# A hardware loop over pairs of quads and 64x64 blocks in the output stage of a gated delta rule

## The reference

```
q = l2norm(q) / sqrt(D); k = l2norm(k)
def step(state, inp):
    q_t, k_t, v_t, a_t, b_t = inp
    state = a_t[..., None, None] * state
    stored = einsum('bhij,bhj->bhi', state, k_t)
    delta = b_t[..., None] * (v_t - stored)
    state = state + einsum('bhi,bhj->bhij', delta, k_t)
    o_t = einsum('bhij,bhj->bhi', state, q_t)
_, outs = scan(step, state0, (qT, kT, vT, aT, bT))
var = mean(out * out, axis=-1)
out = out * rsqrt(var + 1e-06) * rms_w
gate = silu(x @ Wgate)
return out * gate @ Wout
```

## Time and profile before

| | |
|---|---|
| median of three runs | 4024.93 us |
| profiled execution | 4019.74 us |
| its span | 4018.1 us |
| TensorE matmul busy, of the span | 2600.4 us, 65% |
| VectorE, ScalarE, POOL busy | 50%, 33%, 19% |
| mean granted clock of TensorE | 0.722 |

### The profile page before, as it was taken

One profiled execution on the slowest core, in us unless ns is written; L12 is line 12 of the kernel. 1 busy time (PEld: TensorE's weight loads), 2 busy tenths in 40 slices (PEclk: granted clock), 3 DMA queues, 4 the chain that ended last, 5 costly groups with the idle time before them and its releaser, 6 DMA issues. The chain is left out here.

```text
span 4018.1 us, 107610 instructions
## 1 busy us (share of the span) xinstructions
PE 2600.4 (65%) x42132; PEld 1917.5 (48%) x42132; DVE 2017.4 (50%) x5379; ACT 1331.4 (33%) x3117; POOL 780.0 (19%) x1137
## 2 busy tenths in 40 slices
PE   5986776246888845555476278778783009999900
PEld 2554544234555534443244256555562009999900
DVE  3385665734666622225502367667767004444466
ACT  3764454224666633332200043333431002222200
POOL 1221112013555510000000011011110660000066
PEclk8987777555555556667676588888995559999955
DMA  3536474663444434442196721211210522222265
GB/s 109 188 129 244 160 259 169 237 239 95 98 107 98 102 97 146 136 128 107 75 415 248 285 103 56 67 56 55 70 48 33 182 95 66 70 70 70 68 202 167
DMA packets 386623, 537.35 MB, mean 134 GB/s; under 512 B 121244, under 2 KB 314744, under 8 KB 378488
## 3 DMA queue, kind: packets, MB, share of 16 engines
q1 hardware_dynamic: 307672, 343.88, 26.0%
q0 software_dynamic: 58304, 152.42, 11.4%
q10 hardware_dynamic: 20320, 36.44, 2.4%
HBM read 327.58 MB, written 216.15 MB: 135 GB/s over the span
## 5 line engine op out<-in xcount | busy, mean ns | idle before, releaser
L1036 ACT ACTIVATE ss_write_ps<-ss_state,ss_gammas 128x64 f32<-128x64 f32 x1024 | 263.3, 303 | 197.5 <-DVE ss_state L1084 197.5
L448 PE MATMUL dc_rows_ps<-dc_weights,dc_hT 128*128 128x512 f32 x512 | 287.8, 691 | 7.3 <-issue 2.6
L2628 PE MATMUL se_up_ps<-se_xT,se_w 128*128 128x128 f32 x2176 | 267.1, 277 | 0.0
L505 PE MATMUL dc_solve_ps<-dc_sides,dc_blocks 32*32 32x32 f32 x8192 | 124.6, 227 | 216.0 <-ACT dc_blocks L599 101.7
L2636 PE MATMUL se_y_ps<-se_w,se_aT 128*128 128x256 f32 x1088 | 257.3, 380 | 0.0
L2628 PEld LDWEIGHTS se_up_ps<-se_xT,se_w 128*128 128x128 f32 x2176 | 255.6, 193 | 0.4 <-DVE se_w L2693 0.3
L2766 POOL DMA_INDIRECT cb_y<-scratch_ys,cb_to x128 | 137.3, 1073 | 564.9 <-DVE cb_to L2780 526.2
L505 PEld LDWEIGHTS dc_solve_ps<-dc_sides,dc_blocks 32*32 32x32 f32 x8192 | 111.5, 139 | 230.0 <-issue 116.5
L2693 DVE COPY se_w<-mx_weights 128x2048 f32 x136 | 166.8, 1227 | 104.1 <-issue 104.1
L2636 PEld LDWEIGHTS se_y_ps<-se_w,se_aT 128*128 128x128 f32 x1088 | 196.8, 191 | 20.7
L1203 PE MATMUL do_mix_ps<-do_u,do_blocks 32*32 32x16 f32 x8192 | 102.5, 196 | 159.3 <-issue 124.0
(11 more groups left out here) (347 smaller groups left out, 5717.2 us busy)
## 6 DMA issues: line engine op xcount, KB each, us to landing
ex_w<-in_w_all SPq DMA_DIRECT2D x64, 1024.0 KB, 21.1
scratch_rows<-dc_rows POOLq DMA_DIRECT2D x64, 512.0 KB, 4.3
scratch_vw<-dc_out POOLq DMA_DIRECT2D x64, 512.0 KB, 4.2
dc_c_rows<-scratch_rows SPq DMA_DIRECT2D x64, 384.0 KB, 4.5
scratch_xs<-wa_zeros ACTq DMA_DIRECT2D x34, 512.0 KB, 14.6
se_xs<-scratch_xs SPq DMA_DIRECT2D x136, 128.0 KB, 2.1
scratch_ys<-se_y SPq DMA_DIRECT2D x136, 128.0 KB, 1.7
ss_wq_rows<-scratch_vw SPq DMA_DIRECT2D x128, 128.0 KB, 2.3
```

The source lines that it names most:

```text
L448: mm = pe.matmul(to, hT[n % 2][:, k, :], weights[:, k, columns], start=(k == 0), stop=(k == HALVES - 1), skip_group_check=True)
L505: mm = pe.matmul(solve_ps[tokens, :].rearrange("p (a f) -> p a f", a=2)[:, :, h * HEAD:(h + 1) * HEAD], blocks[c % 2][tokens, h, :, :].rea ...
L1036: ins = act.activation(write_ps[b][:, k, 0:WIDTH], state[b][:, k, :], ACT.Copy, scale=gammas[i][:, b, k, c:c + 1])
L2628: mm = pe.matmul(up_ps[i % 2][:, c * P:(c + 1) * P], w[i % (2 * AHEAD)][:, k * DFF + c * P:k * DFF + (c + 1) * P], xT[i % 2][:, k, :], sta ...
```

## The change

The stage's blocks become 64x64: a block holds the products of four chunks on its diagonal. A buffer `blocks` keeps one quad's blocks in the layout partition, tile, chunk of the four, token, head, so that one head's block is read with a step of 16 elements. VectorE sets both buffers to zero once. After that eight DMAs for each quad (one for each chunk of a tile, 16 partitions each) write the products straight into the diagonal, and nothing else is ever written. ScalarE's `make_blocks` and the parity mask go. The mix has 128 matmuls in a quad.

For this the delta stage stores the products with the head innermost: its last product writes into a new tile `qkd_turned` with a step of 16 elements, after the previous group's store of that tile.

`read` gets a semaphore of its own, and is loaded behind the blocks. TensorE's program runs over pairs of quads: for each batch of 8 quads the first pair is written out, and the other three are a hardware loop. `weights_ready` is waited for once, ahead of the first mix. A counter `mix_begun` is incremented in each mix.

```diff
         qkd = sb("qkd", [P, PAIRS])
+        qkd_turned = sb("qkd_turned", [P, T, T, HEADS])
...
-                        sync.wait_ge(qkd_out, 16 * g)
+                        sync.wait_ge(qkd_ready, at(g))
...
-                        pool.dma_start(chunk_rows(d["qkd"], g), qkd[:, :]).then_inc(qkd_out, 16)
+                        pool.dma_start(chunk_rows(d["qkd"], g), qkd_turned[:, :, :, :].rearrange("p s t h -> p (s t h)")).then_inc(qkd_out, 16)
...
-                        seq_b.tell(vec.tensor_tensor(rows_of_pairs(qkd), rows_of_pairs(qkd), over_rows(1), ALU.mult), qkd_ready, g + 1)
+                        if g > 0:
+                            vec.wait_ge(qkd_out, 16 * g)
+                        seq_b.tell(vec.tensor_tensor(qkd_turned[:, :, :, :].rearrange("p s t h -> p s h t"), rows_of_pairs(qkd), over_rows(1), ALU.mult), qkd_ready, g + 1)
...
-        qkd = [sb(f"qkd{i}", [P, Q, DIM]) for i in both]
+        blocks = [sb(f"blocks{i}", [P, Q, SIDE, T, HEADS]) for i in both]
...
-        blocks = [sb(f"blocks{i}", [P, 2, HEADS, 2, T]) for i in both]
...
                     if q >= 2:
                         sync.wait_ge(mixed, at((q - 1) * 2))
+                    sync.dma_start(u[i][:, :, :], quad_rows(d["solved_u"], q)).then_inc(first_in[i], 16)
+                    if q < 2:
+                        sync.wait_ge(cleared, at(q + 1))
+                    for c in range(P // T):
+                        lines = slice(c * T, (c + 1) * T)
+                        sync.dma_start(blocks[i][lines, :, c % SIDE, :, :].rearrange("p n t h -> p n (t h)"), quad_rows(d["qkd"], q)[lines, :, :]).then_inc(first_in[i], 16)
+                    if q >= 2:
                         sync.wait_ge(summed, at((q - 1) * 2))
-                    sync.dma_start(qkd[i][:, :, :], quad_rows(d["qkd"], q)).then_inc(first_in[i], 16)
-                    sync.dma_start(u[i][:, :, :], quad_rows(d["solved_u"], q)).then_inc(first_in[i], 16)
-                    sync.dma_start(read[i][:, :, :], quad_rows(d["solved_q"], q)).then_inc(first_in[i], 16)
+                    sync.dma_start(read[i][:, :, :], quad_rows(d["solved_q"], q)).then_inc(read_in[i], 16)
...
-                def mix(m):
-                    q, half = divmod(m, 2)
+                def mix(pair_of_quads, i, half):
+                    m = pair_of_quads * 4 + i * 2 + half
                     if half == 0:
-                        pe.wait_ge(first_in[q % 2], at((q // 2 + 1) * 48))
-                    pe.wait_ge(blocks_ready, at(m + 1))
-                    if m >= 2:
+                        pe.wait_ge(first_in[i], at((pair_of_quads + 1) * FIRSTS))
+                    if not (isinstance(m, int) and m < 2):
                         pe.wait_ge(summed, at(m - 1))
+                    pe.sem_inc(mix_begun, 1)
                     for n in range(2):
                         for h in range(HEADS):
-                            for j in range(4):
-                                tokens = slice(32 * j, 32 * j + 32)
-                                mm = pe.matmul(mix_ps[m % 2][tokens, n, h * HEAD:(h + 1) * HEAD], blocks[m % 2][tokens, n, h, :, :].rearrange("p c t -> p (c t)"),
-                                               u[q % 2][tokens, half * 2 + n, h * HEAD:(h + 1) * HEAD], start=True, stop=True, skip_group_check=True)
+                            for j in range(P // (SIDE * T)):
+                                tokens = slice(SIDE * T * j, SIDE * T * (j + 1))
+                                mm = pe.matmul(mix_ps[half][tokens, n, h * HEAD:(h + 1) * HEAD], blocks[i][tokens, half * 2 + n, :, :, h].rearrange("p c t -> p (c t)"),
+                                               u[i][tokens, half * 2 + n, h * HEAD:(h + 1) * HEAD], start=True, stop=True, skip_group_check=True)
                     mm.then_inc(mixed, 1)
...
-                def project(m):
-                    pe.wait_ge(weights_ready, at(1))
+                def project(q, half, b):
+                    m = q * 2 + half
                     pe.wait_ge(oT_ready, at(m + 1))
-                    if m >= 2:
+                    if not (isinstance(m, int) and m < 2):
                         pe.wait_ge(x_ready, at(m - 1))
...
-                for q in range(QUADS + 1):
-                    if q < QUADS:
-                        mix(2 * q)
-                        mix(2 * q + 1)
-                    if q > 0:
-                        turn(2 * q - 2)
-                        turn(2 * q - 1)
-                        project(2 * q - 2)
-                        project(2 * q - 1)
+                def finish(q, i, b):
+                    for half in range(2):
+                        turn(q, i, half)
+                    for half in range(2):
+                        project(q, half, b)
+
+                def two_quads(ii, b_before, b):
+                    for half in range(2):
+                        mix(ii, 0, half)
+                    if b_before is not None:
+                        finish(ii * 2 - 1, 1, b_before)
+                    for half in range(2):
+                        mix(ii, 1, half)
+                    finish(ii * 2, 0, b)
+
+                pe.wait_ge(weights_ready, at(1))
+                for b in range(BATCH):
+                    first = b * QUADS_PER_BATCH // 2
+                    two_quads(first, b - 1 if b > 0 else None, b)
+                    with pe.Fori(first + 1, first + QUADS_PER_BATCH // 2) as ii:
+                        two_quads(ii, b, b)
+                finish(QUADS - 1, 1, BATCH - 1)
...
-                def make_blocks(m):
-                    q, half = divmod(m, 2)
-                    if half == 0:
-                        act.wait_ge(first_in[q % 2], at((q // 2 + 1) * 48))
-                    if m >= 2:
-                        act.wait_ge(mixed, at(m - 1))
-                    for par in range(2):
-                        ins = act.activation(blocks[m % 2][:, :, :, par, :].rearrange("p n h t -> p (n h) t"),
-                                             pair_of(qkd[q % 2], half).rearrange("p (a t) -> p a t", t=T), ACT.Copy, scale=parity[:, par:par + 1])
-                    ins.then_inc(blocks_ready, 1)
...
-                make_blocks(0)
-                make_blocks(1)
...
-                    if q + 1 < QUADS:
-                        make_blocks(2 * q + 2)
-                        make_blocks(2 * q + 3)
...
+                for i in both:
+                    vec.memset(blocks[i][:, :, :, :, :], 0.0).then_inc(cleared, 1)
...
+                    if half == 0:
+                        vec.wait_ge(read_in[q % 2], at((q // 2 + 1) * 16))
```

More of the change, by code:

```diff
@@ L1108, in build_delta_outputs @@
     Q = 4
+    SIDE = 4
     QUADS = TILES // Q
@@ L1117, in build_delta_outputs @@
         ident = sb("ident", [P, P])
-        parity = sb("parity", [P, 2])
         w_out = sb("w_out", [P, HALVES, DIM])
@@ L1135, in build_delta_outputs @@
         y_ps = [ps(f"y_ps{i}", [P, 2, DIM]) for i in both]
-        consts, order, weights_ready, blocks_ready, mixed, summed, squared, var_ready, rooted, silued, o_ready = map(sem, (
-            "consts", "order", "weights_ready", "blocks_ready", "mixed", "summed", "squared", "var_ready", "rooted", "silued", "o_ready"))
-        turned, oT_ready, projected, x_ready = map(sem, ("turned", "oT_ready", "projected", "x_ready"))
-        first_in, gate_in, x_in = ([sem(f"{n}{i}") for i in both] for n in ("first_in", "gate_in", "x_in"))
+        consts, order, weights_ready, cleared, mixed, summed, squared, var_ready, rooted, silued, o_ready = map(sem, (
+            "consts", "order", "weights_ready", "cleared", "mixed", "summed", "squared", "var_ready", "rooted", "silued", "o_ready"))
+        turned, oT_ready, projected, x_ready, mix_begun = map(sem, ("turned", "oT_ready", "projected", "x_ready", "mix_begun"))
+        first_in, read_in, gate_in, x_in = ([sem(f"{n}{i}") for i in both] for n in ("first_in", "read_in", "gate_in", "x_in"))
         x_out = [sem.from_zero(f"x_out{i}") for i in both]
-        CONSTS = 16 * (4 + BATCH)
+        CONSTS = 16 * (3 + BATCH)
+        FIRSTS = 16 * (P // T + 1)
         def quad_rows(dram, q):
@@ L1213, in turn @@
                         for k in range(HALVES):
-                            mm = pe.transpose(tr_ps[m % 2][:, n, k, :], o[q % 2][:, half * 2 + n, k * P:(k + 1) * P], ident[:, :])
+                            mm = pe.transpose(tr_ps[half][:, n, k, :], o[i][:, half * 2 + n, k * P:(k + 1) * P], ident[:, :])
                     mm.then_inc(turned, 1)
-                def project(m):
-                    pe.wait_ge(weights_ready, at(1))
+                def project(q, half, b):
+                    m = q * 2 + half
@@ L1219, in project @@
                     pe.wait_ge(oT_ready, at(m + 1))
-                    if m >= 2:
+                    if not (isinstance(m, int) and m < 2):
                         pe.wait_ge(x_ready, at(m - 1))
-                    b = m * BATCH // PAIRS_OF_TILES
                     for n in range(2):
```

(2 more changed lines are left out.)

3 lines of the change are left out of this document (1 added, 2 removed).

## The result

The kernel after takes 3985.71 us (median of 4 runs, 3984.70 to 3990.84) beside 4025.15 of before (4015.74 to 4027.43): ratio 0.9909, 95% interval 0.9891 to 0.9927. That is 39 us faster. The forecast was 17 us faster, 4008 us. Its direction held, and the time lies in its range of 3965 to 4050, but the gain is more than twice the one forecast. The profiled execution took 3984.70 us, its span 3983.1.

A forecast was written before the change was run, and what follows sets the result against it. It took the mix to be bound by its program's arrival, about 3.9 us per packet. Terms of -20 (14 periods), -1 (first mixes), +2 (start) and +2 (delta stage) gave -17 us, so 4008 us, range 3965 to 4050.

The forecast's parts named there:

- item 2: Mix on TensorE: 128 rounds a quad at 118 ns, set by strided weight loads whatever the clock, 15.2 us.
- item 4: Projection on TensorE: runs at either clock, taken as 4.9 us, bounds 3.5 and 6.8.
- item 1: TensorE's loop and halved mixing instructions: instruction loads leave the path, taken at zero; straight-part loads of 8.5 us stay hidden.
- item 3: ScalarE without make_blocks: the copy follows the turn at once, turn to projection 2.08 instead of 3.85 us.
- item 7: Delta stage: products writing with a 64-byte stride cost +2 us (0 to +21), the price being mostly for strided reads.
- the filling: Small term added to the mix in the sum of one period, 0.1 us.
- The first two mixes: Start of the output stage: they take 30.5 in place of 31.52 us, -1.
- the start: Start of the output stage: memsets and eight issues delay the constants about 7 us, 1 kept; together +2 (0 to +7).
- A: Rival on the mix: stride costs nothing, mix 9.0 us, period 16.1, about 3910 us; chance 0.11.
- B: Rival on the mix: two row groups' strided loads obstruct each other, 236 ns a round, about 4248 us; 0.16 with milder forms.
- C: Rival: loop back edges load code (+24) or a wait takes the gain, 4020 to 4035 us; chance 0.10.

The follow-up runs named there:

- before, copies first: Kernel before, with ScalarE copying the turned tile ahead of making the next quad's blocks instead of behind it; 3990.99 us, ratio 0.9935.
- after, passes put back: Kernel after, with ScalarE's four former block-making passes again ahead of the copies of the turned tile, writing a spare buffer; 4029.16 us, ratio 1.0028.
- the constants first: Kernel after, with SyncE issuing ident, w_out, rms_w and ga ahead of the first quad's loads; 3971.91 us, ratio 0.9880.
- the turning on the read: Kernel after with those constants loaded first, and VectorE's last delta-stage product reading qkd over the 64-byte stride and writing contiguous; 3965.24 us, ratio 0.9879.

## Why the prediction was right in its direction and its gain too small

Two steps failed: the price of a round in item 2, 118 ns where 110 was measured, and item 4, which set the projection's time apart from the wait in front of it, 4.9 us where 4.49 was measured. The mechanisms of items 1, 2 and 3 held. Here is one period by its parts, each from its start to the next part's start, as a mean over the 14 periods, in us:

| | before | forecast | after | before, copies first | after, passes put back |
|---|---|---|---|---|---|
| mix | 14.27 | 15.3 | 14.19 | 14.72 | 14.19 |
| turn, to the projection | 4.09 | 2.1 | 1.80 | 2.11 | 3.20 |
| projection, to the mix | 5.40 | 4.9 | 4.49 | 4.85 | 6.30 |
| period | 23.76 | 22.3 | 20.47 | 21.68 | 23.69 |

The mix of the kernel after is no shorter than that of before. Halving the instructions took the packets off its path, and the stride put nearly the same time back. Of the 3.29 us that a period gained, 2.29 lie between turn and projection and 0.91 in the projection.

*The instruction loads* (item 1) were right. There are 14 packets in the 14 periods, none of them in the second and third pass of either loop, and the mix shows no gap for any; the form of the loop does not matter, but the halved count does. (Before has 16 quads of 272 matmuls and transposes in this stage, 4352, and not the 4288 given above.)

*The mix* (item 2) was the right mechanism, a load of 64 strided columns that costs the same at both clocks, and was mis-sized: 118 ns a pair was taken from L1676 and 110 was measured, so the mix is 14.2 us and not 15.2. L1454, which has the change's own distance, had given 110 ns for one record of 128 columns, so 220 for the two that a matmul leaves, and half of that, 110, for 64 columns. I had both and took the one nearer in form; the distance decided. The term is off by 1.0 us a period, the largest single error.

*ScalarE without its passes* (item 3): the copy follows at once, right; 1.80 us instead of the 2.1 taken from the first quad, since half 0 is now copied alone while TensorE turns half 1. The 3.85 us of the quad shown was a little under the mean of before, 4.09.

*The projection* (item 4) is the step whose weight I missed. I took 4.9 us as a property of where the clock happens to be. It is 4.49 after, and the run with the passes put back shows that it does not stand by itself: with 1.4 us more in front of it, it ran at a clock of 0.56 and took 6.4 us. What sets the clock's place in the period stays open.

*The delta stage* (item 7) was allowed 2 us on the ground that the stride's price lies on the read. It does not: the product takes 7.1 us with the stride on the write and 7.1 with it on the read, 4 x 2.7 = 10.8 us of VectorE's time in all. How much of that reached the edited stage the spread between executions hides.

So a period is 1.0 + 0.3 + 0.4 + 0.1 (the filling) = 1.8 us shorter than forecast, which over 14 periods with the unrounded 1.83 is 26 us. The first two mixes are 2 us shorter than forecast, for the same 110 ns. Against it stand the start, +5.4 for +2 (the memset's 3.5 us and eight issues in front of the constants, which I had named as 7 and then cut to 1), and the first issue, +4.5 for item 7's +2, which the spread between executions may hold alone. Sum: -26 - 2 + 3.4 + 2.5 = -22, and with the forecast's -17 the 39 us by which the next stage starts earlier.

With the passes put back the 64x64 blocks give nothing (23.69 beside 23.76), though not by the same parts: the gap is shorter and the projection longer. With them out of the way, both steps give: the order of the copies 2.1 us, the new blocks 1.2 more. I forecast a sum of terms, and the terms are not independent.

*The rivals.* A, a stride without cost, is false: contiguous weights give 3933 us. B, loads in each other's way, is false: 32x32 groups of four take half the time of pairs of 64x64. C is false for this loop and true for one twice as long.

## What to carry to other kernels

Look at the order of work on the engine that TensorE waits for before rebuilding TensorE's program: a new order of calls on ScalarE gave 29 us of the 46. A wait of TensorE can come with more than its own length: with 1.4 us more in front of the projection the period grew by 3.2 us, the rest at a lower clock, so read the granted clock of the part behind the wait too. For strided fp32 weights take the price from a load with the same distance in bytes, and count the instructions of a loop's body before counting on the loop.

The fastest version with the right output is the kernel after with the constants first and the turning on the read, 3965.24 us (ratio 0.9879, 0.9860 to 0.9898); with the constants first alone it is 3971.91 us, and these two can't be told apart.

## What the runs showed of the hardware that I had not expected

- Weights 8 bytes apart load nearly as fast as contiguous ones (60 and 58 ns a pair at full clock, 107 and 107 at half). At 16, 32 and 64 bytes a pair takes 119, 120 and 110 ns; 119 and 110 at either clock, 120 at half, the one that the run has. Of these the farthest is the cheapest.
- Four strided 32-column loads in different row groups overlap like contiguous ones, some 57 ns a group of four.
- A loop body of 2150 instructions on TensorE is loaded again in each pass (69 packets of 16 KB in 14 periods), one of 1100 is not.
- A block DMA of 64 pieces was issued in 0.43 us, one of 256 in 0.61, one of 1024 in 0.67 (medians; the longest of the last took 4.0, and eight in a row 9.16 us). The issue time grows far less than the pieces.
- VectorE's product of 4096 fp32 takes 4.42 us contiguous and 7.1 with 64 bytes between elements, on the read or on the write alike.
